# A state-space recurrence: GpSimd takes one product with C in four, and the states get a fifth slot in the first chunk

## The reference

```python
dA  = jnp.exp(dt[..., None] * A)                       # (.., 1024, 16)
dBx = (dtx[..., :, None] * Bg[..., None, :])            # dtx = dt * x
def step(h, inp):
    dA_i, dBx_i, C_i = inp
    h = dA_i * h + dBx_i
    y = jnp.einsum('bgn,bgcn->bgc', C_i, h...)          # product with C, sum over the 16 states
    return (h, y)
```

## Time and profile before

| | |
|---|---|
| median of 3 runs | 687.64 us (686.48 to 688.21) |
| profiled execution, its own time | 689.65 us |
| its span in the profile | 687.9 us |
| granted TensorE clock, mean | 0.97 of full speed |
| busy: PE, DVE, ACT, POOL | 638.5, 426.4, 344.9, 428.8 us |
| first and last scan (L751) start | 37.4 and 460.6 us |
| DMA | 163.51 MB, mean 238 GB/s |

### The profile page before, as it was taken

The page is one execution under the profiler, slowest core; times in us unless marked ns, Lnnn a source line. Parts: engine busy times, 40 slices in busy tenths (PEclk is TensorE's granted clock), DMA queues, the critical chain, the costliest instruction groups (busy, mean ns, idle before and its releaser), DMA issues.

```text
span 687.9 us, 8630 instructions
## 1 busy us (share of the span) xinstructions
PE 638.5 (93%) x2846; PEld 508.9 (74%) x2846; DVE 426.4 (62%) x660; ACT 344.9 (50%) x657; POOL 428.8 (62%) x244
## 2 busy tenths in 40 slices
PE   4959997799999879999979999999999999899998
PEld 3737764466666557777756777776899999899998
DVE  4078896899888777888995989871323132423132
ACT  4349889348999733323343333422543443543441
POOL 0176773637777899887883888745354564354561
PEclk9989998999999999999997999999999999999999
DMA  8699987379999987989783989733344544143421
GB/s 344 222 355 336 336 276 277 128 232 364 307 347 356 396 303 271 348 324 336 279 333 129 342 313 341 269 124 121 125 152 120 155 124 150 38 151 122 153 66 43
DMA packets 49165, 163.51 MB, mean 238 GB/s; under 512 B 4320, under 2 KB 18528, under 8 KB 48480
## 3 DMA queue, kind: packets, MB, share of 16 engines
q1 hardware_dynamic: 49120, 162.95, 67.5%
HBM read 145.24 MB, written 17.69 MB: 237 GB/s over the span
## 4 chain that ended last, share of the span: by engine, by line
PE 58%; DVE 18%; ACT 11%; issue 5%; DMA 5%; POOL 3%; DVEq 0%; SPq 0%; ACTq 0%; POOLq 0%
PE work L960 43%; PE da L960 13%; DVE da L751 10%; DVE hs L762 4%; DMA bb<-b_rows 4%; ACT da L545 3%; PE work L970 2%; ACT L522 2%; POOL hs L447 2%; ACT L662 1%; DVE gated_n L873 1%; DMA c_rows<-c_rows 1%; DMA sm<-small 1%; ACT L545 1%; ACT sp_w L676 1%
## 5 line engine op out<-in xcount | busy, mean ns | idle before, releaser
L751 DVE TENSOR_TENSOR_SCAN da<-da,hs 128x290 f32<-128x290 f32 (+1 forms) x256 | 198.4, 817 | 43.5 <-POOL hs L447 21.9
L447 POOL TENSOR_TENSOR hs<-dtx,bb 128x1160 f32<-128x1160 f32 (+1 forms) x64 | 171.0, 2673 | 65.4 <-PE work L970 53.7
L545 ACT ACTIVATE da<-dt,a_neg 128x261 f32<-128x261 f32 (+1 forms) x256 | 118.1, 494 | 137.3 <-DVE hs L762 136.6
L426 POOL TENSOR_TENSOR ws<-wraw,ws 128x1024 fp32r<-128x1024 f32 x40 | 101.4, 2535 | 92.9 <-ACT ws L553 92.9
L960 PE MATMUL work<-sq,wraw 128*128 128x290 f32 x512 | 129.0, 414 | 5.1 <-DVE sq L834 3.5
L960 PEld LDWEIGHTS work<-sq,wraw 128*128 128x128 f32 x512 | 98.5, 193 | 35.6 <-issue 6.4
L960 PE MATMUL work<-hn,win 128*128 128x290 f32 (+1 forms) x336 | 102.6, 454 | 12.3 <-DVE hn L825 8.0
L762 DVE TENSOR_TENSOR hs<-da,cb 128x580 f32<-128x580 f32 (+1 forms) x128 | 105.3, 822 | 10.6 <-DMA cb<-c_rows 3.7
L960 PEld LDWEIGHTS work<-hn,win 128*128 128x128 f32 x336 | 65.1, 198 | 45.6 <-issue 18.8
L553 ACT CAST ws<-wraw 128x1024 fp32r<-128x1024 f32 x48 | 50.3, 1049 | 70.5 <-PE work L960 36.0
L960 PE MATMUL work<-hn,ws 128*128 128x350 f32 x456 | 75.3, 323 | 1.6 <-DVE hn L921 1.6
(11 more groups left out here) (108 smaller groups left out, 662.3 us busy)
## 6 DMA issues: line engine op xcount, KB each, us to landing
wraw<-w_stream SPq DMA_DIRECT2D x104, 512.0 KB, 4.3
bb<-b_rows SPq DMA_DIRECT2D x32, 700.0 KB, 6.8
cb<-c_rows SPq DMA_DIRECT2D x32, 700.0 KB, 4.7
bb<-b_rows SPq DMA_DIRECT2D x32, 580.0 KB, 8.5
cb<-c_rows SPq DMA_DIRECT2D x32, 580.0 KB, 6.6
c_rows<-c_rows SPq DMA_DIRECT2D x8, 875.0 KB, 11.0
c_rows<-c_rows SPq DMA_DIRECT2D x8, 725.0 KB, 6.8
win<-w_in SPq DMA_DIRECT2D x4, 1024.0 KB, 13.4
```

Of the source, the lines that this page charges most:

```text
L426: nc.gpsimd.tensor_tensor(ws[:, k % NW, 1, :], wraw[:, split_loads[k] % NRAW, :], ws[:, k % NW, 0, :].bitcast(F32), ALU.subtract).then_inc ...
L447: nc.gpsimd.tensor_tensor(hs[:, u % NH, 0:NQ * n].rearrange("p (n t) -> p n t", t=n), dtx[:, t % 2, 0:n].unsqueeze(1).to_broadcast([P, NQ, ...
L545: last = nc.scalar.activation(dst, src, ACT.Exp, scale=a_neg[:, j:j + 1])
L751: nc.vector.tensor_tensor_scan(da[:, k % ND, 0:w], da[:, k % ND, 0:w], hs[:, u % NH, p * w:(p + 1) * w], 0.0, ALU.mult, ALU.add).then_inc( ...
```

## The change

In the first chunk, units with q = 1 are handled otherwise. DVE scans their states into `hs` in place of `da` (the decay is still read from `da`), and makes no product. POOL multiplies all four states by C in `hs` with one operation of 4 x 290 = 1160 columns (`times_c` in POOL's stream), in slot u+1, behind `input_term(u+2)` and ahead of the softplus of that slot. The decays that take over the unit's `da` buffers wait for its scans, each for its own. PE's sum and `load_c(u+3)` wait for POOL's product. `hs` has five slots of 1160 columns in the first chunk and four of 1400 in the second, over the same columns (5800 in place of 5600). So `input_term(u)` of the first chunk waits for the sum of unit u-5; units 32 to 35 wait for the sums of units 28, 29, 31 and 31.

```diff
+HS = 5 * NQ * TS[0]
-NH, NB, ND, NC = 4, 4, 4, 3
+NB, ND, NC = 4, 4, 3
+
+NH = (5, 4)
+FIRST_SLOT = (0, 2)
...
+def slot_at(u):
+
+    c = u // UNITS
+    return (u % UNITS + FIRST_SLOT[c]) % NH[c] * NQ * TS[c]
...
+def on_pool(u):
+
+    return u < UNITS and u % QU == 1
...
 def recurrence(u):
 
+    if on_pool(u):
+        return [("scan", u, p) for p in range(4)]
     return [("scan", u, 0), ("scan", u, 1), ("times_c", u, 0), ("scan", u, 2), ("scan", u, 3), ("times_c", u, 1)]
...
+        def multiplied(eng, u):
+
+            if on_pool(u):
+                eng.wait_ge(c_times_pool, u // QU + 1)
+            else:
+                eng.wait_ge(c_times, products_through(u))
@@ SP, load_c
                 if u >= NC:
-                    sp.wait_ge(c_times, products_through(u - NC))
+                    multiplied(sp, u - NC)
@@ POOL
-                if u >= NH:
-                    v = u - NH
-                    if v < UNITS:
-                        pool.wait_ge(h_summed, v + 1)
...
+                v = slot_before(u)
+                if v is not None and v < UNITS:
+                    pool.wait_ge(h_summed, v + 1)
...
+            def times_c(u):
+                c, w = u // UNITS, NQ * TS[u // UNITS]
+                pool.wait_ge(c_loaded[u % NC], 16 * (u // NC + 1))
+                pool.wait_ge(scan_done, piece(u, NQ - 1) + 1)
+                nc.gpsimd.tensor_tensor(states(u, 0, w), states(u, 0, w), cb[:, u % NC, 0:w], ALU.mult).then_inc(c_times_pool, 1)
...
                 if unit is not None and unit + 1 < NCH * UNITS:
                     input_term(unit + 1)
+                if unit is not None and unit >= 1 and on_pool(unit - 1):
+                    times_c(unit - 1)
@@ ACT, decay
-                if k >= ND:
-                    act.wait_ge(c_times, (k - ND) // 2 + 1)
+
+                if k >= ND and on_pool(piece_of(k - ND)[0]):
+                    act.wait_ge(scan_done, k - ND + 1)
+                elif k >= ND:
+                    v, j = piece_of(k - ND)
+                    act.wait_ge(c_times, products_through(v) - 1 + j)
@@ DVE, scan
-                nc.vector.tensor_tensor_scan(da[:, k % ND, 0:w], da[:, k % ND, 0:w], hs[:, u % NH, p * w:(p + 1) * w], 0.0,
+                dst = states(u, p * w, (p + 1) * w) if on_pool(u) else da[:, k % ND, 0:w]
+                nc.vector.tensor_tensor_scan(dst, da[:, k % ND, 0:w], states(u, p * w, (p + 1) * w), 0.0,
@@ PE, state_sum
-                pe.wait_ge(c_times, products_through(u))
+                multiplied(pe, u)
```

More of the change, by code:

```diff
@@ L39 @@
 PIECE0 = [sum(UNITS * n for n in NP[:c]) for c in range(NCH)]
-PRODUCTS = UNITS * sum(NP) // 2
 IN_DT, IN_X, IN_B, IN_CZ = 0, 1, 3, 5
@@ L72, in unit_of, with slot_before, ends @@
     return u // UNITS, u % UNITS // QU, u % QU
+def slot_at(u):
+    c = u // UNITS
+    return (u % UNITS + FIRST_SLOT[c]) % NH[c] * NQ * TS[c]
+def slot_before(u):
+    def ends(v):
+        return slot_at(v) + NQ * TS[v // UNITS]
+    shared = [v for v in range(u) if slot_at(v) < ends(u) and slot_at(u) < ends(v)]
+    return max(shared, default=None)
 def piece(u, p):
@@ L77, in piece, with piece_of @@
     return PIECE0[c] + u % UNITS * NP[c] + p
+def piece_of(k):
+    u = k // NP[0]
+    return (u, k % NP[0] // 2) if u < UNITS else (UNITS + (k - PIECE0[1]) // NP[1], (k - PIECE0[1]) % NP[1] // 2)
+def on_pool(u):
+    return u < UNITS and u % QU == 1
 def products_through(u):
-    return piece(u, NP[u // UNITS] - 1) // 2 + 1
+    return 2 * len([v for v in range(u + 1) if not on_pool(v)])
+PRODUCTS = products_through(NCH * UNITS - 1)
 def recurrence(u):
+    if on_pool(u):
+        return [("scan", u, p) for p in range(4)]
     return [("scan", u, 0), ("scan", u, 1), ("times_c", u, 0), ("scan", u, 2), ("scan", u, 3), ("times_c", u, 1)]
@@ L224, in build @@
         with ExitStack() as scanned:
-            hs = sb("hs", [P, NH, NQ * TM], stack=scanned)
+            hs = sb("hs", [P, HS], stack=scanned)
             cb = sb("cb", [P, NC, NQ * TM], stack=scanned)
@@ L228, in build @@
         hn2 = sb("hn2", [P, 2, KD, TM], F32R)
-        sb("cb_beyond_hn2", [P, NC * NQ * TM - 2 * KD * TM])
+        sb("cb_beyond_hn2", [P, HS + NC * NQ * TM - 2 * (HH + KD) * TM])
         with ExitStack() as prep:
@@ L267, in build @@
         added, h_summed, skip_done, y_done = sem("added"), sem("h_summed"), sem("skip_done"), sem("y_done")
+        c_times_pool = sem("c_times_pool")
         y_summed = sem("y_summed")
@@ L294, in small_ap, with states @@
             return sm[:, col + i:col + i + 1]
+        def states(u, lo, hi):
+            return hs[:, slot_at(u) + lo:slot_at(u) + hi]
+        def multiplied(eng, u):
[3 more added lines that the diff above has]
+                eng.wait_ge(c_times, products_through(u))
         def h(c, k):
@@ L440, in input_term @@
                 pool.wait_ge(bb_loaded[u % NB], 16 * (u // NB + 1))
-                if u >= NH:
-                    v = u - NH
-                    if v < UNITS:
-                        pool.wait_ge(h_summed, v + 1)
-                    else:
-                        pool.wait_ge(added, adds_through(v + 1 if v % QU == 0 else v))
-                nc.gpsimd.tensor_tensor(hs[:, u % NH, 0:NQ * n].rearrange("p (n t) -> p n t", t=n),
+                v = slot_before(u)
+                if v is not None and v < UNITS:
+                    pool.wait_ge(h_summed, v + 1)
+                elif v is not None:
+                    pool.wait_ge(added, adds_through(v + 1 if v % QU == 0 else v))
+                nc.gpsimd.tensor_tensor(states(u, 0, NQ * n).rearrange("p (n t) -> p n t", t=n),
                                         dtx[:, t % 2, 0:n].unsqueeze(1).to_broadcast([P, NQ, n]),
@@ L456, in add_states @@
                 w = 2 * TS[c]
-                lo, hi = hs[:, u % NH, 0:w], hs[:, u % NH, w:2 * w]
-                pool.wait_ge(c_times, products_through(u))
+                lo, hi = states(u, 0, w), states(u, w, 2 * w)
+                multiplied(pool, u)
                 if q <= 1:
@@ L467, in add_states @@
                     pool.wait_ge(added, n - 1)
-                    nc.gpsimd.tensor_tensor(total, hs[:, (u - 1) % NH, 0:w], lo, ALU.add).then_inc(added, 1)
+                    nc.gpsimd.tensor_tensor(total, states(u - 1, 0, w), lo, ALU.add).then_inc(added, 1)
                 else:
@@ L757, in times_c @@
                 w = GS[c] * TS[c]
-                here = slice(2 * j * w, 2 * (j + 1) * w)
+                lo, hi = 2 * j * w, 2 * (j + 1) * w
                 if j == 0:
@@ L761, in times_c @@
                 dve.wait_ge(scan_done, k + 2)
-                nc.vector.tensor_tensor(hs[:, u % NH, here].rearrange("p (i w) -> p i w", w=w), da[:, k % ND:k % ND + 2, 0:w],
-                                        cb[:, u % NC, here].rearrange("p (i w) -> p i w", w=w), ALU.mult).then_inc(c_times, 1)
+                nc.vector.tensor_tensor(states(u, lo, hi).rearrange("p (i w) -> p i w", w=w), da[:, k % ND:k % ND + 2, 0:w],
+                                        cb[:, u % NC, lo:hi].rearrange("p (i w) -> p i w", w=w), ALU.mult).then_inc(c_times, 1)
             def gate_y(t):
@@ L967, in state_sum @@
                     pe.wait_ge(y_done, m)
-                pe.wait_ge(c_times, products_through(u))
+                multiplied(pe, u)
                 for i in range(NQ):
-                    last = nc.tensor.matmul(work[SUM][:, 0:n], sm[:, S_IDENT:S_IDENT + P], hs[:, u % NH, i * n:(i + 1) * n],
+                    last = nc.tensor.matmul(work[SUM][:, 0:n], sm[:, S_IDENT:S_IDENT + P], states(u, i * n, (i + 1) * n),
                                             start=(q == 0 and i == 0), stop=(q == QU - 1 and i == NQ - 1))
```

## The result

The changed kernel takes 689.01 us in the median of 12 runs (686.38 to 691.89), the kernel before 687.07 us beside it (12 runs, 685.33 to 688.21). The ratio is 1.0036, 95% interval 1.0020 to 1.0052: 1.4 to 3.6 us slower. The forecast was +1.7 us.

The account below looks back on a forecast made before the run. PE was taken to set the pace from 134 to 203.5 us, ACT to hold DVE up in the rounds before. Start +0.6 and load_c(32) +1.1 gave +1.7 us, from 687.64 to 689.3 us; range 683 to 693 us.

Parts of the forecast that it names:

- PE sets the pace from 134 to 203.5 us: In that window PE is busy 68.8 of 69.5 us, so DVE's products can't set the pace.
- DVE's saving at q = 1 ends in a wait for ACT: At units 5, 9, 13, 25, 29 the next unit waits for ACT anyway: gain 0 of 1.44 us each.
- POOL's product, 2.80 us: Each 1160-column product on POOL was priced at 2.80 us, bounds 2.44 to 3.1; eight make 22.4 us.
- The start, +0.6 us: Near 50 us, unit 1's product delays POOL's softplus, then ACT's softplus block by 0.85 us and unit 6: +0.6 us.
- load_c(32), +1.1 us: Unit 29's POOL product makes load_c(32) later, ahead of six weight transfers with DMA full, delaying PE at 232 us: +1.1 us.
- unit 21's gain: Unit 22 can start at ACT's decay, at 159.06 in place of 159.94 us: 0.9 us, carried to unit 29.
- The input term of unit 34 at nothing: It waits for unit 31's sum, 2 to 3 us later, but unit 34's scans follow a product waiting for DMA: 0.
- 1 (-11.5 us): Rival: DVE is the bound, so eight units pay 1.44 us each: -11.5 us, 676.1 us; chance 0.08.
- 2 (-4.3 us): Rival: at units 1, 17 and 21 the 1.44 us each reach the end: -4.3 us, 683.3 us; chance 0.15.
- 3: Rival: nothing reaches the end; ACT catches up after the start, DMA's full stretch doesn't move: -1.5 to +0.5 us; chance 0.15.
- 4: Rival: late C rows in every round, 1.1 us more at each of units 21, 25, 29: +5 us, 692.6 us; chance 0.20.

Follow-up runs that it names:

- e5: The changed kernel with units 1 and 29 back on DVE (POOL products for units 5, 9, 13, 17, 21, 25): 688.56 us against 687.71, ratio 1.0010.
- e6: The changed kernel with POOL products for units 6, 10, 14, 18, 22, 26 (q = 2) instead: 683.19 us against 687.71 for the kernel before, ratio 0.9933.
- e3: The changed kernel with only unit 1's product on POOL, five slots kept: 689.65 us, ratio 1.0011 to the kernel before.
- e9: The kernel before, with only load_c(32) waiting for one product more: 691.44 us against 687.63, ratio 1.0062.
- e7: The changed kernel with six weight transfers moved from behind load_c(32), two by two behind load_c(34), (35), (36): 688.10 us, ratio 1.0005 to the kernel before.
- e8: The kernel before with six weight transfers moved from behind load_c(32), two by two behind load_c(34), (35), (36): 684.52 us against 687.71, ratio 0.9968.
- e1: The changed kernel with unit 29's product back on DVE, seven left on POOL: 688.22 us against 688.90 for the kernel before, ratio 0.9992.
- e10: The kernel before, with load_c(8), (12), (16), (20), (24), (28) each waiting for one product more: 687.93 us against 687.63, ratio 1.0022.

## Why the prediction was right

**The direction and the size.** +1.7 us forecast, 1.4 to 3.6 measured. The mechanism of the larger term was right and is shown. That the size fits so well is partly luck: the sum rested on two terms, of which the first (+0.6 us) was over its size and can't be seen by the norm, and the second (+1.1 us) came out at 2.1 us.

**PE sets the pace from 134 to 203.5 us.** Right: DVE lost 5 us of work there and PE's stretch kept its 69 us. e5 excludes DVE as the bound.

**DVE's saving at q = 1 ends in a wait for ACT.** Right, and the step that explains most: DVE's waits for decays rose from 11.6 to 24.1 us, unit 6 to unit 10 is 20.63 us in both traces, and e6, with the same saving one unit later, is 4.6 us faster.

**POOL's product, 2.80 us.** It measured 2.65 us. The Trainium skill's 2.6 cycles an element (GPSIMD Engine Reference, Elementwise — side-by-side cycle accounting) had given an estimate of 2.5 us; the measured one lies between the two. The advice of the Trainium skill (GPSIMD Engine Reference, Engine selection) to keep such work on VectorE fits the changed kernel's result, but not e6, 4.6 us faster with the same exchange: the place decides.

**The start, +0.6 us.** The wait is there (1.42 us at 50.87 us), but the stretch to unit 6 grew by 0.21 us only. Counted from the first scan, ACT's block starts at 15.20 us (50.87 - 35.67), and before at 14.78 (52.20 - 37.42): 0.42 us later, where I had +0.85. The block starts when POOL's softplus is through. That softplus starts 2.33 us later than before (12.70 us from the first scan against 10.37) and not 2.80: POOL's input terms of units 2 and 3, which wait for their B rows in both traces, began 0.27 us sooner after the first scan (5.31 us, before 5.58), and the product was 0.15 us shorter. As a time, e3 couldn't show the start's share, and by the norm nothing of it is left to see.

**load_c(32), +1.1 us.** The mechanism was right (e9), the term was too small: 69.36 - 67.25 = 2.1 us. From the last scan's end to the issue it was 0.83 us (200.45 to 201.28) and became 3.52 (197.93 to 201.45). I had counted 2.80 for it. What is missing is POOL's: the product stands behind the input term of unit 31, which had waited 3.18 us for B rows, so it started 0.86 us after the last scan; of this, 0.15 us came back as it took 2.65 us. And unit 21's gain was 0.6 us (unit 22 came 2.52 us ahead of before's, in a trace 1.94 ahead), not 0.9.

**The input term of unit 34 at nothing.** Right in the changed kernel, where DMA hides it; e7 takes the cover away, and its trace is 2.9 us behind e8's at the next norm, of which the chain from this term explains 1.3 us of waiting and the clock takes 1.6. I had named the cover, and not its price.

**Rivals.** 1 (-11.5 us) and 2 (-4.3 us) are excluded by the result itself, 1.4 to 3.6 us slower, and 1 by e5 as well. 3 had at most +0.5 us; load_c(32) did move by 2.1 us, and e9 shows that such a move reaches the end. 4 is excluded by the traces: with seven products on POOL (e1) or six transfers late (e10) no product of the first chunk's rounds waits for C rows. e1's time, at most +0.9 us, leaves no room for it either. The times of e5 and e10 alone don't exclude it.

## What to carry to other kernels

Before work is taken off an engine, look at what releases the next instruction behind it: if another engine does, the saving becomes a wait, and the same saving one unit on may be worth its full size. When work moves to another engine, follow every queue that waits for its result: here a load with six unrelated transfers behind it, at the head of a stretch in which DMA is full. And compare the traces of two kernels from event to event, not end to end.

## What the runs showed of the hardware

The time of one and the same program goes with the mean granted TensorE clock of the run: in the kernel before (33 runs), 688.3 to 689.4 us at 0.972 and 684.1 to 684.2 us at 0.982, which is more than the change under study. Behind a wait PE's clock can be at the lower of its two levels: eight products took 3.82 us at 0.51 of full speed after PE had waited 2.32 us (e7), and 2.19 us at full speed after 1.05 us (e8). A scan costs about the same into SBUF (745 ns) as into PSUM (753 ns).
